# Nine small VectorE instructions placed ahead of one large one at each chunk boundary

## The chip, the cores and the metric

The kernel runs on one NeuronCore of one Trainium2 chip. The metric is device time in microseconds (us), median of the runs of one kernel. The engines are named as in the profile: PE is TensorE, DVE is VectorE, ACT is ScalarE, POOL is GpSimd, SP is SyncE; PEld is TensorE's weight load. Each engine takes its own instructions in the order in which they are written, and semaphores make it wait for others.

## The reference

128 samples of 750 x 32 values are cut into 92 overlapping patches each, embedded to 128 features, and sent through attention with 8 heads and a mixture of 8 experts of which each token uses 2. Cut to what matters:

```
h = patches(x) @ W + b                                # 128 x 92 tokens of 128 features
a = attention(layernorm(h))                           # 8 heads; a_flat is (tokens, 1024)
h = h + (a_flat @ Wlt)                                # the projection
t = layernorm(h)
logits = t @ Wr + br                                  # 8 experts
gates = softmax(logits); top 2, renormalised
out = h + sum over the 2 chosen e of gate_e * (relu(t @ W1[e] + b1[e]) @ W2[e] + b2[e])
```

## The kernel before, in words

It runs in four stages. The first computes embedding and attention, and leaves the attention result in device memory. The second, which the change touches, projects it, adds the residual, normalises, picks the two experts of each token and scatters the token rows to a sorted place in memory. The third runs the experts over tiles of 512 sorted rows, the fourth adds up.

The second stage takes the 11,776 tokens in 23 chunks of 512, numbered 0 to 22. Chunks 0 to 8 are written out, 9 to 20 are two chunks each in a loop that runs six times, 21 and 22 are written out again. While the chunk function works on chunk c, it also prepares and projects chunk c + 1:

- PE turns eight 512 x 128 blocks of chunk c + 1 (turn_a, L1546) and projects each one two places later (project). Blocks 0 to 5 are projected as high and low half, with three matmuls each (L342 to L344); blocks 6 and 7 in full precision (L1555). Between them stand the expert counts of chunk c - 1 (count, L1579 and L1581), and the turned residual and the logits of chunk c (turn_h L1566, logits L1573).
- ACT copies a turned block from PSUM as the rounded high half aT_h (L907), and makes the normalised rows trow (L924), the squares (L914) and the exponential for the gates (L937).
- DVE subtracts to get the low half aT_l (keep_aTl, L1147), adds the residual (keep_h1, L1157; the profile writes the tile as h), forms gates and row numbers of chunk c - 1 (weigh, L1223 to L1226, and rows_of, L1231 to L1236), and then runs the choice of experts for chunk c, a chain of small dependent instructions from L1183 to L1213 (shift, lg, top, eq, key, one, mask_line, upto).
- POOL scatters the rows of chunk c - 1 by eight indirect DMAs (L756), and takes the power for the deviation (root2, L747).

The waits around the change: PE's project(c + 1, 0) waits for the first low half; weigh waits for ACT's exponential and rows_of for PE's count; POOL's scatter waits for rows_of's last result posi (L1236); ACT's squares wait for DVE's lean (L1163); POOL's root2 waits for DVE's varB (L1168); DVE's shift (L1183) waits for root2. PE's turn_h waits for keep_h1, and keep_h1 waits for the last projection of its chunk. Every two chunks the transfers of arow and hch start as soon as keep_h1 has read hch.

Of the kernel before, what the change touches and what calls it, by code (L numbers as in the profile page):

```python
# [44 lines left out]
HL = 6  # L45
# [28 lines left out]
def at_least(eng, sem, value):  # L74

    if isinstance(value, int) and value <= 0:
        return
    eng.wait_ge(sem, value)
# [19 lines left out]
def build(nc, x, tok_w, tok_b, wq, wk, wv, wlt, wr, br, w1, b1, w2, b2, out):  # L98
# [8 lines left out]
    with ExitStack() as ctx, nc.allow_non_contiguous_dma("biases once"):  # L107
# [905 lines left out]
        def _(dve):  # L1013
# [130 lines left out]
            def keep_aTl(c, j):  # L1144
                at_least(dve, aTh_kept, AC * c + j + 1)
                at_least(dve, proj_done, AC * c + j - TURNS + 1)
                V.tensor_tensor(aT_l[:, j % TURNS], turn_ps[j % TURNS][:], aT_h[:, j % TURNS].bitcast(F32),  # L1147
                                ALU.subtract).then_inc(aTl_kept, 1)

            def keep_h1(c, i, q):  # L1150
                at_least(dve, proj_done, AC * (c + 1))
                if isinstance(c, int):
                    dve.wait_ge(a_in[q], 32 * (c // 2 + 1))
                else:
                    dve.wait_ge(a_in[q], 16 * (c - q + 2))
                at_least(dve, res_done, c - 1)
                V.tensor_tensor(h1[:, q].rearrange("d (r p) -> d r p", r=RT), proj_ps[:].rearrange("d (r p) -> d r p", r=RT),  # L1157
                                hch[q][:].rearrange("d (p r) -> d r p", r=RT), ALU.add).then_inc(h1_kept, 1)

            def keep_lean(c):  # L1160
                at_least(dve, lg_done, c + 1)
                at_least(dve, square_kept, 2 * c)
                V.tensor_copy(lean[:].unsqueeze(2), lg_ps[:, :, NE:NE + 1]).then_inc(lean_kept, 1)  # L1163

            def keep_var2(c):
                at_least(dve, square_kept, 2 * c + 2)
                at_least(dve, rstd2_kept, c)
                V.tensor_scalar(varB[:], varB[:], EPS, None, ALU.add).then_inc(var2_kept, 1)  # L1168
# [10 lines left out]
            def take_logits(c, q):  # L1179
                step_no[0] = 0  # L1180
                at_least(dve, trow_kept, 2 * c - 2)
                at_least(dve, rstd2_kept, c + 1)
                V.scalar_tensor_tensor(shift[:, q], lean[:], D ** 0.5, rstdB[:, q], ALU.mult, ALU.mult).then_inc(shift_kept, 1)  # L1183
                link(c, V.tensor_tensor(lg[:], lg_ps[:, :, 0:NE], wide(rstdB[:, q]), ALU.mult))
                link(c, V.tensor_tensor(lg[:], lg[:], brs[:].unsqueeze(1).to_broadcast([P, RT, NE]), ALU.add))

            def largest(c, which):

                m = top[:, which]
                link(c, V.tensor_reduce(m, lg[:], AX_X, ALU.max))  # L1190
                link(c, V.tensor_tensor(eq[:], lg[:], wide(m), ALU.is_equal))

            def first_of_equals(c, which):

                kk = top[:, 4 + which]
                link(c, V.tensor_tensor(key[:], eq[:], rank[:], ALU.mult))
                link(c, V.tensor_reduce(kk, key[:], AX_X, ALU.max))
                link(c, V.tensor_tensor(one[:, 1 - which], rank[:], wide(kk), ALU.is_equal))

            def without_first(c):  # L1200
                link(c, V.scalar_tensor_tensor(lg[:], one[:, 1], -3.0e38, lg[:], ALU.mult, ALU.add))

            def chosen(c):
                at_least(dve, count_done, c)
                step_no[0] += 1
                V.tensor_tensor(mask, one[:, 0], one[:, 1], ALU.add).then_inc(route, 1)
                V.tensor_tensor(top[:, 2], top[:, 1], top[:, 0], ALU.subtract).then_inc(gap_kept, 1)
                dve.wait_ge(route, NR * c + step_no[0])
                line = mask_line[:].bitcast(F32)
                windows = bass.AP(tensor=line.tensor, offset=line.offset,  # L1210
                                  ap=[list(line.ap[0]), [NE, RT], [1, NE], [NE, RT]])
                with nc.allow_low_precision("whole numbers up to 4"):
                    V.tensor_reduce(upto[:], windows, AX_X, ALU.add).then_inc(mask_kept, 1)  # L1213

            def weigh(c, q):

                at_least(dve, gapexp_kept, c + 1)
                at_least(dve, scattered[q], 16 * 2 * RT * (c // 2) if isinstance(c, int) else 8 * 2 * RT * (c - q))
                dve.wait_ge(goal_kept, SETUP)
                gate = [trow[:, q, choice, :, D + 1:D + 2] for choice in (0, 1)]  # L1220
                ratio = top[:, 3].unsqueeze(2)
                mine = trow[:, q, :, :, D:D + 1].bitcast(I32)
                link(c, V.tensor_scalar(top[:, 6], top[:, 3], 1.0, None, ALU.add))  # L1223
                link(c, V.reciprocal(gate[1], top[:, 6].unsqueeze(2)))
                V.tensor_scalar(mine, mine, 2 * CT, None, ALU.add)
                V.tensor_tensor(gate[0], gate[1], ratio, ALU.mult)  # L1226

            def rows_of(c, q):

                at_least(dve, count_done, c + 1)  # L1230
                link(c, V.tensor_tensor(place[:], count_ps[:, 64:64 + RT * NE].rearrange("p (r e) -> p r e", r=RT),  # L1231
                                        base[:].unsqueeze(1).to_broadcast([P, RT, NE]), ALU.add))
                link(c, V.tensor_tensor(base[:], count_ps[:, 64 + RT * NE:64 + (RT + 1) * NE], base[:], ALU.add))
                link(c, V.tensor_tensor(seat[:], one[:], place[:].unsqueeze(1).to_broadcast([P, 2, RT, NE]), ALU.mult))
                link(c, V.tensor_reduce(posf[:], seat[:], AX_X, ALU.add))
                V.tensor_copy(posi[:, q], posf[:]).then_inc(posi_kept, 1)  # L1236
# [11 lines left out]
            def first_tiles_ready():  # L1248

                lined = [0]  # L1250

                def nxt(ins):
                    lined[0] += 1
                    ins.then_inc(ready_kept, 1)
                    dve.wait_ge(ready_kept, lined[0])

                nxt(V.tensor_tensor(held[:], base[0:1], ebase[0:1], ALU.subtract))
                nxt(V.tensor_reduce(least[:, 0:1], held[:], AX_X, ALU.min))
                nxt(V.tensor_scalar(least[:, 1:2], least[:, 0:1], float(TT), -16.0 * 2 * RT, ALU.is_ge, ALU.mult))
                for half in (0, 1):  # L1260
                    V.tensor_scalar(ready[:, half:half + 1], least[:, 1:2], 16.0 * 2 * RT * ((NCH + 1 - half) // 2), None,
                                    ALU.add).then_inc(ready_kept, 1)
# [3 lines left out]
            def chunk(c, i, q, more):  # L1266
                after_first = not isinstance(c, int) or c > 0
                keep_h1(c, i, q)
                for j in range(AC):
                    if j == 4:  # L1270
                        keep_var2(c)
                    if more and j < HL:
                        keep_aTl(c + 1, j)
                    if j == 0 and after_first:
                        step_no[0] = CHOSEN
                        weigh(c - 1, 1 - q)
                        rows_of(c - 1, 1 - q)
                        if isinstance(c, int) and c == NCH - 2:
                            first_tiles_ready()
                        assert step_no[0] == NR, step_no  # L1280
                    if j == 1:
                        keep_lean(c)
                    if isinstance(c, int) and 1 <= c <= NE and j == 2:
                        dve.wait_ge(high_kept, NE + c)
                        V.tensor_tensor(w2split[:, c - 1, :, 1], w2raw[:, c - 1, :, 1], w2split[:, c - 1, :, 0].bitcast(F32),
                                        ALU.subtract).then_inc(low_kept, 1)
                    if j == 5:
                        take_logits(c, q)
                        largest(c, 0)
                    if j == 6:  # L1290
                        first_of_equals(c, 0)
                        without_first(c)
                        largest(c, 1)
                    if j == AC - 1:
                        first_of_equals(c, 1)
                        chosen(c)
                        assert step_no[0] == CHOSEN, step_no
# [395 lines left out]
```

## Time and profile before

| what | value |
|---|---|
| median of 3 runs | 1533.73 us (1533.18 to 1535.3) |
| the profiled execution's own time | 1533.04 us |
| its span in the trace | 1530.9 us |
| second stage in the trace, first to last keep_h1 | 843.19 to 1109.46 us |
| busy in the span: PE, PEld, DVE, ACT, POOL | 92%, 74%, 77%, 66%, 52% |
| mean granted TensorE clock | 0.963 |

The profile is of one execution, whose span is 2.1 us shorter than its own time. Shares of busy time are averages over four stages with different limits, so a change in the second is read from rows of the second. In a row of the timeline stand the start, the duration, the engine, the line, the operation with its tiles, and in brackets the idle time of the engine before it with what ended it.

### The profile page before, as it was taken

The page shows a single profiled execution, that of the slowest core. Times are in us where ns is not written, and L with a number is a line of the kernel's source. Part 1 is how long each engine was busy: PE and PEld are TensorE (multiplying, and loading weights), DVE is VectorE, ACT ScalarE, POOL GpSimd, SP SyncE. Part 2 cuts the span into 40 slices and gives each one's busy share as a digit, 9 for nine tenths or more (in the row PEclk, how much of TensorE's full clock was granted, in tenths as well). Part 3 has the DMA queues.
Part 4 walks back from the last instruction along what each step waited for, and adds up shares of the span by engine and source line. Part 5 has one row for each costly group of instructions (what it writes and reads, how often), then busy time and mean ns, then how long its engine had stood idle before and what let it go on. Part 6 is the DMA issues. An engine that isn't in the chain of part 4 may idle for free.

```text
span 1530.9 us, 31767 instructions
## 1 busy us (share of the span) xinstructions
PE 1401.2 (92%) x7902; PEld 1132.8 (74%) x7902; DVE 1180.4 (77%) x3082; ACT 1017.2 (66%) x2282; POOL 801.9 (52%) x891
## 2 busy tenths in 40 slices
PE   4899999999999999999998999999969999999930
PEld 3687888887888888888886777777758888888820
DVE  1899898988989898898995688888856666666633
ACT  1587887878788788888885677777745555555510
POOL 1476443444444444444442377777765666666665
PEclk8999999999999999999998999999979999999975
DMA  3322222222223222222224887777477777777667
GB/s 83 131 75 90 76 101 81 89 84 78 89 74 107 79 85 86 77 89 83 100 106 162 290 267 268 241 256 254 171 274 243 248 247 246 247 245 247 244 211 297
DMA packets 115925, 249.58 MB, mean 163 GB/s; under 512 B 15504, under 2 KB 70944, under 8 KB 112928
## 3 DMA queue, kind: packets, MB, share of 16 engines
q1 hardware_dynamic: 94640, 209.63, 38.6%
q0 software_dynamic: 14368, 32.25, 6.6%
q10 hardware_dynamic: 6864, 7.09, 1.3%
q8 instruction: 22, 0.36, 0.1%
q14 instruction: 31, 0.25, 0.1%
HBM read 100.78 MB, written 92.56 MB: 126 GB/s over the span
## 4 chain that ended last, share of the span: by engine, by line
PE 73%; DMA 9%; DVE 6%; issue 5%; POOL 4%; ACT 2%; SPq 1%; POOLq 0%; DVEq 0%; ACTq 0%
PE bank L342 16%; PE bank L344 15%; PE bank L343 15%; PE bank L1481 9%; PE bank L1414 5%; PE bank L1506 5%; DMA hch<-h_scratch 3%; DMA sorted_scratch<-trow,posi 2%; POOL sorted_scratch L756 2%; PE bank L1404 2%; PE bank L1618 2%; PE bank L1643 1%; DMA out_dram<-outs 1%; PE bank L1546 1%; PE bank L1422 1%
## 5 line engine op out<-in xcount | busy, mean ns | idle before, releaser
L628 POOL TENSOR_TENSOR prob<-expo,inv 92x368 f32<-92x368 f32 x256 | 204.6, 799 | 422.6 <-DVE inv L1106 422.6
L783 POOL DMA_INDIRECT y_scratch<-ytok,tin x212 | 205.0, 967 | 137.6 <-issue 72.1
L1351 DVE SCALAR_TENSOR_TENSOR hid_l<-bank,hid_h 128x512 fp32r<-128x512 f32 x212 | 146.4, 691 | 128.6 <-ACT hid_h L969 125.3
L969 ACT ACTIVATE hid_h<-bank 128x512 fp32r<-128x512 f32 x212 | 126.7, 598 | 149.3 <-PE bank L344 149.3
L756 POOL DMA_INDIRECT sorted_scratch<-trow,posi x184 | 180.4, 980 | 71.4 <-issue 62.6
L1481 PE MATMUL bank<-z,xnT 128*92 128x368 f32 x512 | 200.3, 473 | 0.0
L1099 DVE TENSOR_REDUCE peak<-bank 92x4 f32<-92x368 f32 x256 | 136.3, 532 | 77.5 <-PE bank L1481 77.4
L830 ACT ACTIVATE z<-bank 128x368 f32<-128x368 f32 x256 | 122.0, 477 | 66.7 <-PE bank L344 59.2
L868 ACT ACTIVATE w2s<-bank 128x368 fp32r<-128x368 f32 x256 | 122.4, 478 | 45.8 <-PE bank L344 41.1
L875 ACT ACTIVATE expo<-cent 92x368 f32<-92x368 f32 x256 | 130.2, 508 | 31.4 <-DVE cent L1111 28.9
L1126 DVE TENSOR_TENSOR w2s<-bank,w2s 128x368 fp32r<-128x368 f32 x256 | 136.2, 532 | 5.4 <-ACT w2s L868 2.5
L1111 DVE TENSOR_TENSOR cent<-bank,peak 92x368 f32<-92x368 f32 x256 | 136.6, 533 | 1.0
L1119 DVE TENSOR_TENSOR probT_l<-bank,probT_h 92x368 fp32r<-92x368 f32 x256 | 134.9, 527 | 1.8 <-ACT probT_h L856 1.8
L1092 DVE TENSOR_REDUCE total<-expo 92x4 f32<-92x368 f32 x256 | 133.6, 522 | 0.5 <-ACT expo L875 0.3
L884 ACT ACTIVATE val<-bank 128x368 f32<-128x368 f32 x256 | 120.4, 470 | 17.8 <-PE bank L344 16.6
L1506 PE MATMUL bank<-ident,prob 92*92 92x92 f32 x1024 | 123.0, 242 | 0.3 <-POOL prob L628 0.3
L342 PE MATMUL bank<-probT_h,xtok_h 92*128 92x368 f32 x256 | 114.1, 446 | 9.9 <-DVE w2s L1126 7.1
L856 ACT ACTIVATE probT_h<-bank 92x368 fp32r<-92x368 f32 x256 | 119.8, 468 | 0.3
L1546 PE MATMUL bank<-ident,arow 128*128 128x128 f32 x736 | 114.7, 280 | 4.5 <-DMA hch<-h_scratch 4.4
L1506 PEld LDWEIGHTS bank<-ident,prob 92*92 92x92 f32 x1024 | 103.4, 124 | 18.5 <-issue 5.5
L1546 PEld LDWEIGHTS bank<-ident,arow 128*128 128x128 f32 x736 | 91.3, 146 | 34.6 <-DMA hch<-h_scratch 11.7
L1147 DVE TENSOR_TENSOR aT_l<-bank,aT_h 128x512 fp32r<-128x512 f32 x138 | 94.7, 691 | 27.4 <-ACT aT_h L907 25.5
(193 smaller groups left out, 3803.0 us busy)
## 6 DMA issues: line engine op xcount, KB each, us to landing
ax_scratch<-val SPq DMA_DIRECT2D x64, 736.0 KB, 3.5
arow<-ax_scratch SPq DMA_DIRECT2D x23, 2048.0 KB
w1t<-w1s SPq DMA_DIRECT2D x53, 512.0 KB, 3.5
w2t<-w2s SPq DMA_DIRECT2D x53, 512.0 KB, 3.1
tin<-sorted_scratch SPq DMA_DIRECT2D x53, 260.0 KB, 3.0
xin<-in_x_dram SPq DMA_DIRECT2D x32, 372.0 KB
yearly<-y_scratch SPq DMA_DIRECT2D x24, 256.0 KB, 9.0
h_scratch<-hT SPq DMA_DIRECT2D x32, 184.0 KB, 7.1
```

Of the source, the lines that this page charges most:

```text
L342: mm(dst, wh, vh, start=start, stop=False)
L343: mm(dst, wh, vl, start=False, stop=False)
L344: return mm(dst, wl, vh, start=False, stop=stop)
L628: nc.gpsimd.tensor_tensor(prob[:, k % 2], expo[:, k % 2], inv[:, k % 2].unsqueeze(2).to_broadcast([S, HH, S]), ALU.mult).then_inc(prob_kep ...
L756: pool.indirect_dma_start(out=sorted_dram, out_offset=bass.IndirectOffsetOnAxis(ap=posi[:, q, choice, r:r + 1], axis=0), in_=trow[:, q, ch ...
L783: pool.indirect_dma_start(out=y_dram, out_offset=bass.IndirectOffsetOnAxis(ap=tin[:, b, r, D:D + 1].bitcast(I32), axis=0), in_=ytok[:, b % ...
L1099: V.tensor_reduce(peak[:, k % 2], sc, AX_X, ALU.max).then_inc(peak_kept, 1)
L1111: V.tensor_tensor(cent[:, k % 2], sc, peak[:, k % 2].unsqueeze(2).to_broadcast([S, HH, S]), ALU.subtract).then_inc(cent_kept, 1)
L1351: V.scalar_tensor_tensor(hid_l[:, f], hid_ps[f][:], 0.0, hid_h[:, f].bitcast(F32), ALU.max, ALU.subtract).then_inc(hidl_kept, 1)
L1481: mm(score_ps[k % 2][0:S, 0:GT], xnT[:, q, b * S:(b + 1) * S], z[:, b, half * HH:(half + 1) * HH, :], start=True, stop=True).then_inc(scor ...
L1506: ins = nc.tensor.transpose(probT_ps[kt % 2][0:S, m * S:(m + 1) * S], prob[:, kt % 2, m], ident[0:S, 0:S])
L1546: ins = nc.tensor.transpose(turn_ps[j % TURNS][:, r * P:(r + 1) * P], arow[q][:, r, j * P:(j + 1) * P], ident[:])
```

## The change

At the start of the chunk function on VectorE, the subtraction for block 0 of the next chunk is issued after weigh and rows_of instead of ahead of them. Blocks 1 to 5 stay where they are. Line numbers behind it grow by two.

```
@@ -1269,7 +1269,7 @@
                 for j in range(AC):
                     if j == 4:
                         keep_var2(c)
-                    if more and j < HL:
+                    if more and 0 < j < HL:
                         keep_aTl(c + 1, j)
                     if j == 0 and after_first:
                         step_no[0] = CHOSEN
@@ -1278,6 +1278,8 @@
                         if isinstance(c, int) and c == NCH - 2:
                             first_tiles_ready()
                         assert step_no[0] == NR, step_no
+                    if more and j == 0:
+                        keep_aTl(c + 1, j)
                     if j == 1:
                         keep_lean(c)
```

The first place is VectorE at the start of an early chunk, before the change. The row with h is keep_h1, the aT_l rows are low halves of blocks 0 and 1.

```order
L1213 TENSOR_REDUCE upto<-mask_line 128x32
L1157 TENSOR_TENSOR h<-bank,hch 128x512
L1147 TENSOR_TENSOR aT_l<-bank,aT_h 128x512
L1223 TENSOR_SCALAR top<-top 128x4
L1224 RECIPROCAL trow<-top 128x4
L1225 TENSOR_SCALAR trow<-trow 128x8
L1226 TENSOR_TENSOR trow<-trow,top 128x4
L1231 TENSOR_TENSOR place<-bank,base 128x32
L1233 TENSOR_TENSOR base<-bank,base 128x8
L1234 TENSOR_TENSOR seat<-one,place 128x64
L1235 TENSOR_REDUCE posf<-seat 128x8
L1236 CAST posi<-posf 128x8
```

The same place with the change:

```order
L1157 TENSOR_TENSOR h<-bank,hch 128x512
L1223 TENSOR_SCALAR top<-top 128x4
L1224 RECIPROCAL trow<-top 128x4
L1225 TENSOR_SCALAR trow<-trow 128x8
L1226 TENSOR_TENSOR trow<-trow,top 128x4
L1231 TENSOR_TENSOR place<-bank,base 128x32
L1233 TENSOR_TENSOR base<-bank,base 128x8
L1234 TENSOR_TENSOR seat<-one,place 128x64
L1235 TENSOR_REDUCE posf<-seat 128x8
L1236 CAST posi<-posf 128x8
L1147 TENSOR_TENSOR aT_l<-bank,aT_h 128x512 x2
L1163 COPY lean<-bank 128x4
```

Block 0's low half has moved behind nine small instructions and now stands directly before block 1's (the x2); h, lean and all that follows keep their order. This holds for chunks 1 to 21: chunk 0 has no gates to form, and chunk 22 has no next chunk.

The second place is VectorE at the start of chunk 21, before the change, where the four lines of first_tiles_ready (held, least, ready) follow rows_of:

```order
L1236 CAST posi<-posf 128x8
L1257 TENSOR_TENSOR held<-base,ebase 1x8
L1258 TENSOR_REDUCE least<-held 1x1
L1259 TENSOR_SCALAR least<-least 1x1
L1261 TENSOR_SCALAR ready<-least 1x1 x2
L1147 TENSOR_TENSOR aT_l<-bank,aT_h 128x512
L1163 COPY lean<-bank 128x4
```

And with the change:

```order
L1236 CAST posi<-posf 128x8
L1257 TENSOR_TENSOR held<-base,ebase 1x8
L1258 TENSOR_REDUCE least<-held 1x1
L1259 TENSOR_SCALAR least<-least 1x1
L1261 TENSOR_SCALAR ready<-least 1x1 x2
L1147 TENSOR_TENSOR aT_l<-bank,aT_h 128x512 x2
L1163 COPY lean<-bank 128x4
```

In chunk 21 block 0's low half stands behind these five instructions too. On PE, ACT, POOL and SP the order is unchanged.

## Rows read from the trace of the kernel before

**Rows 1.** Two stretches; busy of PE, PEld, DVE, ACT, POOL; clock; DMA share, GB/s:
```profile
869.00:884.00 15.00, 14.62 (x72) 12.29 (x73) 11.21 (x38) 9.46 (x25) 10.73 (x12) 0.77 0.68 233
955.00:1037.00 82.00, 78.42 (x476) 61.64 (x475) 68.93 (x244) 59.35 (x152) 62.09 (x70) 1.00 0.69 246
```

**Rows 2.** Timeline of DVE, chunk 9 and on to chunk 11:
```profile
955.62 1.08 DVE L1157 TENSOR_TENSOR h<-bank,hch 128x512 f32<-128x512 f32 x1
956.68 0.69 DVE L1147 TENSOR_TENSOR aT_l<-bank,aT_h 128x512 fp32r<-128x512 f32 x1
957.29 0.16 DVE L1223 TENSOR_SCALAR top<-top 128x4 f32<-128x4 f32 x1
...
958.97 0.69 DVE L1147 TENSOR_TENSOR aT_l<-bank,aT_h 128x512 fp32r<-128x512 f32 x1
...
962.27 1.36 DVE L1147 TENSOR_TENSOR aT_l<-bank,aT_h 128x512 fp32r<-128x512 f32 x2 [0.31 <-ACT aT_h L907]
963.59 0.16 DVE L1183 SCALAR_TENSOR_TENSOR shift<-lean,rstdB 128x4 f32<-128x4 f32 x1
...
967.18 1.08 DVE L1157 TENSOR_TENSOR h<-bank,hch 128x512 f32<-128x512 f32 x1
...
979.04 1.08 DVE L1157 TENSOR_TENSOR h<-bank,hch 128x512 f32<-128x512 f32 x1 [0.31 <-issue]
```

**Rows 3.** Timeline of PE, chunk 9:
```profile
956.95 0.63 PE L1566 MATMUL bank<-ident,h 128*128 128x128 f32 x4 [0.39 <-DVE h L1157]
...
958.62 0.48 PE L342 MATMUL bank<-aT_h,wlt_h 128*128 128x512 f32 x1
...
959.75 0.48 PE L342 MATMUL bank<-aT_h,wlt_h 128*128 128x512 f32 x1
...
961.67 0.60 PE L1546 MATMUL bank<-ident,arow 128*128 128x128 f32 x4
```

**Rows 4.** Timeline of ACT, chunk 9, the copies of blocks 4 and 5:
```profile
961.63 1.29 ACT L907 ACTIVATE aT_h<-bank 128x512 fp32r<-128x512 f32 x2
```

**Rows 5.** Timeline of DVE, start of chunk 22:
```profile
1109.46 1.04 DVE L1157 TENSOR_TENSOR h<-bank,hch 128x512 f32<-128x512 f32 x1
1110.42 0.16 DVE L1223 TENSOR_SCALAR top<-top 128x4 f32<-128x4 f32 x1
```

**Rows 6.** Timelines of PE in chunks 2 and 7, DVE and PE in chunk 13:
```profile
873.90 0.78 PE L342 MATMUL bank<-aT_h,wlt_h 128*128 128x512 f32 x1
...
934.84 0.48 PE L342 MATMUL bank<-aT_h,wlt_h 128*128 128x512 f32 x1
...
936.42 0.47 PE L342 MATMUL bank<-aT_h,wlt_h 128*128 128x512 f32 x1 [0.21 <-DVE aT_l L1147]
...
1005.58 0.48 PE L342 MATMUL bank<-aT_h,wlt_h 128*128 128x512 f32 x1
...
1006.34 0.69 DVE L1147 TENSOR_TENSOR aT_l<-bank,aT_h 128x512 fp32r<-128x512 f32 x1
...
1007.08 0.50 PE L342 MATMUL bank<-aT_h,wlt_h 128*128 128x512 f32 x1
```

**Rows 7.** Who waited for the low halves L1147 (us, times):
```profile
  PE bank L342: 1.4, 5
  PEld bank L342: 0.6, 2
```

**Rows 8.** Timeline of DVE: shift in chunks 1, 5 and 21:
```profile
865.71 0.16 DVE L1183 SCALAR_TENSOR_TENSOR shift<-lean,rstdB 128x4 f32<-128x4 f32 x1 [3.30 <-POOL rstdB L747]
...
916.07 0.16 DVE L1183 SCALAR_TENSOR_TENSOR shift<-lean,rstdB 128x4 f32<-128x4 f32 x1 [0.56 <-POOL rstdB L747]
...
1105.93 0.16 DVE L1183 SCALAR_TENSOR_TENSOR shift<-lean,rstdB 128x4 f32<-128x4 f32 x1 [0.87 <-POOL rstdB L747]
```

**Rows 9.** Timeline of POOL: root2 in chunk 10:
```profile
973.88 1.04 POOL L747 TENSOR_TENSOR rstdB<-varB,power 128x4 f32<-128x4 f32 x1 [0.27 <-DVE varB L1168]
```

**Rows 10.** Instructions on posi: engines sat idle before them until (us, times):
```profile
  DVE posi L1236: 3.8, 5
```

More of the change, by code:

```diff
@@ L1271, in chunk @@
                         keep_var2(c)
-                    if more and j < HL:
+                    if more and 0 < j < HL:
                         keep_aTl(c + 1, j)
@@ L1280, in chunk @@
                         assert step_no[0] == NR, step_no
+                    if more and j == 0:
+                        keep_aTl(c + 1, j)
                     if j == 1:
```

## The prediction

> **What bounds the kernel now.** I read the table of stretches first: from 955 to 1037 us, which are seven chunks of the second stage, PE is busy for 78.42 of 82 us at a granted clock of 1.00, DVE for 84%, POOL for 76% [rows 1]. No engine is full, so the stage is set by a loop of waits, and I looked for it in the timelines of one chunk. The reader is to follow chunk 9 [rows 2 to 4]. keep_h1 starts at 955.62. PE's turn_h waits for it and starts at 956.95, 1.33 behind; then come the logits and one more turn, and PE reaches project 0 at 958.62, 3.00 behind the start of keep_h1. From there PE runs without a gap to the turn of block 5, 961.67 to 962.27; ACT has copied that block by 961.63 + 1.29 = 962.92; DVE's low half of it starts in the same instant (962.27 + 0.69 = 962.96) and ends at 963.63; shift starts at 963.59 with no idle time before it, and the chain of small instructions runs to the next keep_h1 at 967.18, which shows no idle time either. So the loop closes: 3.00 from keep_h1 to project 0 and 8.56 from project 0 to the next keep_h1, 11.56 in all, with DVE at work for the last 4.2 us of it (962.96 to 967.18). Of each pair in the loop the second step to the next pair costs 0.30 more, which stands in front of keep_h1 as issue time at the branch (979.04 - 967.18 = 11.86) [rows 2].
>
> The low half of block 0 is not on that loop today: it ends at 956.68 + 0.69 = 957.37, and PE comes for it at 958.62. It has 1.25 us to spare [rows 2, 3].
>
> **The change, part by part.** It adds no instruction and no transfer; it moves one DVE instruction of 0.69 us behind nine small ones.
>
> 1. The nine small ones go from 957.29 to 958.97, the start of the next large one: 1.68 us [rows 2]. The low half of block 0 is late by this, less what it frees.
>
> 2. When do the nine start without the low half ahead of them? Chunk 22 has no next chunk and shows it already: L1223 follows keep_h1 at 1110.42 - 1109.46 = 0.96 [rows 5]. In the loop the first instruction after keep_h1 stands at 956.68 - 955.62 = 1.06 [rows 2]. I take 1.03, between the two.
>
> 3. The low half of block 0 then ends 1.03 + 1.68 + 0.69 = 3.40 behind the start of keep_h1. PE needs some 0.05 more: in chunk 13, where PE waits for the low half of block 1, that ends at 1006.34 + 0.69 = 1007.03 and PE starts at 1007.08 [rows 6]. So project 0 starts at 3.45 instead of 3.00: **PE is late by 0.45 us per chunk.** The 1.25 us to spare are used up, and 1.70 - 1.25 gives the same 0.45. The bounds are 0.38 (0.96 at the start) and 0.51 (PE needing 0.08 more and 1.06 at the start).
>
> 4. Does it come back later in the chunk? Behind project 0 PE has no idle time in which to catch up, so the turn of block 5 ends at 962.72 instead of 962.27. ACT had its copy of block 4 behind it by then (961.63 + 0.65), so its copy of block 5 ends at about 963.35, and DVE's low half at 964.08 instead of 963.63. shift starts as much later, and so does the next keep_h1. Nothing in the chain from shift to upto waits, so nothing gives. PE's own way, project 0 to last projection to keep_h1, is delayed alike. The loop becomes 12.01.
>
> 5. What keeps its time: the low half of block 1 ends where it did, since the sum of the work ahead of it is the same; lean, the squares, varB and root2 hang on it and stay at their distance from keep_h1. Posi comes about 0.61 us earlier (the distance between 956.68 and 957.29), so POOL may scatter sooner. POOL waited for posi 5 times, 3.8 us in all [rows 10], but its root2 is held by varB, not by the scatters, in most chunks of the loop (0.27 idle in front of it) [rows 9]. Earlier scatters are therefore worth nothing there. Behind the moved instruction on DVE nothing is queued that gets later; behind PE's new wait is everything PE does in the chunk, and ACT and DVE wait for that.
>
> 6. The new wait replaces older ones. PE already waited 7 times for a low half, 2.0 us together [rows 7], always at block 1: the low half of block 0 stood waiting for ACT and pushed the nine and block 1 back. In chunk 7 project 1 follows project 0 by 936.42 - 934.84 = 1.58, against 959.75 - 958.62 = 1.13 in chunk 9: 0.45 lost. In chunk 13 it is 1007.08 - 1005.58 = 1.50, 0.37 lost [rows 3, 6]. With the nine in front, that wait of DVE is filled, and the loss at block 1 goes.
>
> The sum over the 21 chunks from 1 to 21:
> - Chunks 1 and 2: nothing. In chunk 1 shift waits 3.30 us for POOL [rows 8]. In chunk 2 PE runs at a lower granted clock (0.77 over the stretch) and comes to project 0 only at 873.90, when block 0's low half would long be there [rows 1, 6].
> - Chunks 3 to 8: about nothing together. Chunk 3 pays 0.45. In chunk 4 the input transfer is late and the nine fill DVE's wait, which I estimate to give the 0.45 back. In chunks 5 and 6 shift waits 0.56 for POOL (one of two such rows) [rows 8], which covers 0.45. Chunks 7 and 8 lose 0.45 at block 1 now, and lose it at block 0 then.
> - Chunks 9 to 19: 11 x 0.45 = 4.95, less 0.37 in chunk 13 and about 0.2 in chunk 16 (a wait of the same kind, half as long) = 4.4 us.
> - Chunks 20 and 21: chunk 20 pays 0.45. In chunk 21 five more instructions stand ahead of block 0, but shift waits 0.87 for POOL there [rows 8], which takes back chunk 20's delay. Net nothing. After it POOL leads to the end of the stage, and all later work is shifted by the same amount.
>
> The sum is +4.4 us on the profiled 1533.04, which is 1537.4. That execution was 0.7 us under the median of 1533.73, so against the median I expect 1533.73 + 4.4 = 1538.1.
>
> **A rule against the change.** PE gets a fresh pause of some 0.45 us in every chunk. From 955 to 1037 PE idles for 3.6 of 82 us in short pauses at a granted clock of 1.00, its full level of 2.4 GHz; chunk 2, from 869 on, has 0.77, part of it at 1.2 GHz [rows 1]. The Trainium skill, TensorE: Matmul & The Clock Gate, section A second HAM failure mode: psum-queue depth-cycling, says that small idle times between groups of matmuls, if frequent, can make the clock swing between full and half. By that rule each chunk could cost far more than its 0.45 us. The trace so far speaks against it. It is the last rival below, priced from rows.
>
> **The rivals.**
> - *Full price.* Each of the 21 chunks pays, nothing is hidden: 21 x 0.45 = 9.5 us, 1543.2. For it: the loop is closed, and a later chunk could lose what an earlier one saved. Against it: the waits for POOL and for block 1 stand in the trace.
> - *Hidden.* PE makes up the 0.45, because ACT and DVE find the blocks later than they need them, or POOL's scatters set the pace: 1533 to 1535, say 1534. For it: ACT's copy of block 5 and DVE's low half before it end within 0.04 us of each other, so small shifts may vanish. Against it: this slack is 0.04, not 0.45, and root2 waits for varB.
> - *Faster: the filled wait decides.* The place is the boundary where ACT's copy of block 0 is late because its trow rows waited for scatters. There the nine run in DVE's idle time, posi comes earlier, the scatters end earlier, and the next trow rows do too. It would give the 2.0 us of PE's waits [rows 7] and at most the 3.8 us of POOL's waits [rows 10]; I price it at 2.5 us, 1531.2. It decides if more than half of the chunks start with a late block 0. For it: seven chunks show the wait. Against it: in the other fourteen there is nothing to fill, and these pay.
> - *The clock falls.* Chunk 2, at the lower clock, shows the size: its L342 takes 0.78 against 0.48 [rows 3, 6]. 18 such matmuls by 0.30 in 18 chunks are over 90 us if it stayed so; a fifth of that is 1553.
>
> **How the numbers follow.** Forecast 0.57, full price 0.14, hidden 0.18, faster 0.09, clock 0.02. The likeliest gives 1538.1, with its own range from 1536.3 to 1540. A measurement of this kernel tells about 0.2% from no change, 3.1 us: slower means above 1536.8, faster below 1530.7. Of the forecast 0.52 lies above 1536.8 and 0.05 below it; with full price and clock, slower is 0.68. Same is 0.05 + 0.18 + some of the faster case (its 2.5 us is inside the bound), 0.24. Faster is 0.08. The range for 8 in 10 runs from 1533.2, which takes in most of the hidden case, to 1543.0, which takes in most of the full price.
>
> **What would show it.** In the profile after, in a loop chunk: L1225 (the old L1223) starts about 1.0 behind keep_h1; the low half of block 0 about 2.7 behind; project 0 at 3.45 with a bracket of PE waiting for aT_l, in about 11 or more chunks; keep_h1 to keep_h1 12.0 and 12.3 in turn instead of 11.56 and 11.86; posi 2.5 behind keep_h1 instead of 3.2. The last keep_h1 is 4.4 us later than 1109.46. PE's waits for block 1, POOL's long waits for root2's input excepted, are gone. Step 4 is wrong if project 0 is late but keep_h1 keeps its 11.56; step 3 is wrong if project 0 stays at 3.0; step 6 is wrong if chunks 4, 7, 8 and 13 each grow by 0.45. The prediction fails if the second stage changes by less than 3 or more than 7 us, or if stages one, three or four move.

## The result, and the profile after

The changed kernel takes 1538.7 us (median of 16 runs, 1535.19 to 1544.06), the kernel before 1533.86 us (16 runs, 1530.05 to 1547.6). The ratio is 1.0029, 95% interval 1.0016 to 1.0042: slower by 0.3%. The forecast was 1538.1 in a range of 1533.2 to 1543.0. One slow run (1634.47 us at a mean clock of 0.831, of the kernel with the change in chunks 1 to 8 alone) is left out of the ratios below.

The profiled execution with the change has a span of 1533.1 us, 2.2 more than before. That is less than the times say, and the two spans cut at the first and the last keep_h1 show why. The columns are us, busy us (and instructions) of PE, PEld, DVE, ACT and POOL, granted clock, DMA share and GB/s; the first row is the second stage before, the second row is the same stage with the change.

```profile
843.19:1109.46 266.27, 251.24 (x1494) 196.38 (x1491) 220.32 (x774) 192.32 (x492) 189.40 (x201) 0.99 0.72 251
841.82:1113.98 272.16, 253.35 (x1494) 197.15 (x1491) 219.50 (x774) 193.97 (x492) 190.56 (x201) 0.99 0.69 245
```

The instructions are the same in number and busy for nearly the same time, in a stage that is 5.9 us longer. What lies ahead of it was 1.4 us shorter in this execution and what follows 2.3 us, 3.7 in all. Two executions of the kernel before differ there by 1.3 and 0.7 us, and in the two further profiles with the change the first keep_h1 is at 842.85 and 842.11, with 421.7 and 421.4 us behind the last against 421.4 before. So this is scatter, and I compare the second stage by itself.

The timeline of DVE in chunk 9, with the change, answers to [rows 2]:

```profile
955.91 1.09 DVE L1157 TENSOR_TENSOR h<-bank,hch 128x512 f32<-128x512 f32 x1
956.90 0.17 DVE L1223 TENSOR_SCALAR top<-top 128x4 f32<-128x4 f32 x1
...
958.59 1.29 DVE L1147 TENSOR_TENSOR aT_l<-bank,aT_h 128x512 fp32r<-128x512 f32 x2
959.79 0.15 DVE L1163 COPY lean<-bank 128x4 f32<-128x4 f32 x1
...
963.68 0.69 DVE L1147 TENSOR_TENSOR aT_l<-bank,aT_h 128x512 fp32r<-128x512 f32 x1 [0.39 <-ACT aT_h L907]
964.29 0.15 DVE L1183 SCALAR_TENSOR_TENSOR shift<-lean,rstdB 128x4 f32<-128x4 f32 x1
...
967.91 1.12 DVE L1157 TENSOR_TENSOR h<-bank,hch 128x512 f32<-128x512 f32 x1
...
980.29 1.10 DVE L1157 TENSOR_TENSOR h<-bank,hch 128x512 f32<-128x512 f32 x1 [0.32 <-issue]
```

The nine small instructions start 0.99 behind keep_h1, the low half of block 0 2.68 behind, and the steps are 12.00 and 12.38 us where they were 11.56 and 11.86. In front of block 5's low half there is now a wait of 0.39 for ACT where there was none. PE and ACT in the same chunk, answering to [rows 3, 4]:

```profile
957.24 0.63 PE L1568 MATMUL bank<-ident,h 128*128 128x128 f32 x4 [0.39 <-DVE h L1157]
...
959.33 0.50 PE L342 MATMUL bank<-aT_h,wlt_h 128*128 128x512 f32 x1 [0.18 <-DVE aT_l L1147]
...
963.04 0.60 ACT L907 ACTIVATE aT_h<-bank 128x512 fp32r<-128x512 f32 x1 [0.48 <-PE bank L1548]
```

turn_h is where it was, 1.33 behind keep_h1. project 0 has a wait for the low half in front of it and stands at 3.42. The bracket says 0.18 only, because it counts from the modelled end of the turn ahead; the start is what counts. ACT, whose copies of blocks 4 and 5 were back to back, now waits 0.48 for PE ahead of block 5: the delay travels from PE through ACT to DVE's chain, as the steps of the prediction say. The view of who waited for the low halves has these lines in place of the two of [rows 7]:

```profile
  PE bank L342: 6.5, 19
  PEld bank L342: 5.5, 12
```

By the first line, PE waits in nineteen of the 21 chunks, at block 0 and no longer at block 1. The two others are chunk 2 and chunk 4. In every looped chunk project 1 now follows project 0 by 1.15 to 1.17 us.

The parts of the stage in all profiled executions, in us from keep_h1 to keep_h1, and what was timed (the ratio is to runs of the kernel before on the same chip):

| kernel | chunks 0-2 | 3-8 | 9-20 | 21 | falls of the clock in 9-20 | ratio (95%) |
|---|---|---|---|---|---|---|
| before | 40.2 | 72.2 | 140.7 | 13.1 | 0 | |
| before, again | 40.0 | 71.5 | 140.6 | 13.0 | 0 | |
| with the change | 40.1 | 74.0 | 145.6 | 12.5 | 0 | 1.0029 (1.0016 to 1.0042) |
| with the change, again | 41.6 | 72.1 | 148.7 | 12.5 | 2 | |
| with the change, third | 39.9 | 73.1 | 147.2 | 12.5 | 1 | 1.003 (1.0016 to 1.0043) |
| behind four of nine | 39.7 | 71.1 | 140.3 | 13.1 | 0 | 0.9993 (0.9973 to 1.0013) |
| behind seven of nine | 40.2 | 71.6 | 142.7 | 13.2 | 0 | 1.0003 (0.9985 to 1.0022) |
| change in 9 to 20 alone | 40.4 | 74.5 | 146.3 | 13.1 | 0 | 1.0049 (1.0023 to 1.0076) |
| change in 1 to 8 alone | 40.2 | 71.5 | 140.9 | 13.0 | 0 | 0.9998 (0.9974 to 1.0021) |
| change in 21 alone | 40.3 | 75.6 | 140.3 | 12.6 | 0 | |
| change, PE one turn later | 40.3 | 71.0 | 139.9 | 12.6 | 0 | 0.9968 (0.9951 to 0.9986) |
| before, PE one turn later | 40.1 | 71.5 | 140.8 | 13.0 | 0 | 0.9991 (0.9978 to 1.0003) |
| the last version below | 38.0 | 70.2 | 138.6 | 13.2 | 0 | 0.996 (0.9941 to 0.9979) |

Two kernels have a fall in chunks 3 to 8, each after a long wait of PE for a late input: it is in the 74.5 of the change in 9 to 20 alone (chunk 4 takes 16.22) and in the 75.6 of the change in 21 alone (chunk 7 takes 16.04). The 41.6 is chunk 2 with 15.56 instead of 14.18, because the granted clock stayed low there for some 10 us instead of 7.

### The profile page after: what moved, and what is told of

It reads as the page before. It is cut to its first block, busy times and chain, and to the rows that moved or that the text cites. A ratio compares the mean times of both kernels' runs of the same rounds, so it can differ in the third digit from the quotient of the medians.

```text
span 1533.1 us, 31767 instructions
## 1 busy us (share of the span) xinstructions
PE 1402.5 (91%) x7902; PEld 1133.1 (74%) x7902; DVE 1183.1 (77%) x3082; ACT 1020.0 (67%) x2282; POOL 804.0 (52%) x891
## 4 chain that ended last, share of the span: by engine, by line
PE 76%; DVE 10%; DMA 6%; issue 4%; ACT 2%; POOL 1%; SPq 1%; DVEq 0%; POOLq 0%; ACTq 0%
PE bank L342 17%; PE bank L344 15%; PE bank L343 15%; PE bank L1483 9%; PE bank L1416 5%; PE bank L1508 5%; PE bank L1548 2%; PE bank L1406 2%; PE bank L1620 2%; PE bank L1645 1%; DMA xin<-in_x_dram 1%; DMA out_dram<-outs 1%; DMA yearly<-y_scratch 1%; DVE aT_l L1147 1%; DMA hch<-h_scratch 1%
## 5 line engine op out<-in xcount | busy, mean ns | idle before, releaser
L342 PE MATMUL bank<-probT_h,xtok_h 92*128 92x368 f32 x256 | 114.1, 446 | 9.8 <-DVE w2s L1126 7.1
L1147 DVE TENSOR_TENSOR aT_l<-bank,aT_h 128x512 fp32r<-128x512 f32 x138 | 93.1, 689 | 35.0 <-ACT aT_h L907 28.0
```

Of the source, the lines that this page charges most:

```text
L342: mm(dst, wh, vh, start=start, stop=False)
```

## The experiments

**How far two executions differ.** The kernel before, unchanged.

> The kernel before, unchanged, profiled once more: how far do two executions differ? Theory: the loop chunks 9 to 20 take 140.7 us within 0.5, since a loop of fixed durations sets them; chunks 3 to 8 differ by up to 1.5 us, since input transfers end some of their waits; the first, third and fourth stage differ by 1 to 3 us, which is the scatter between runs. Rival: the loop chunks scatter as much as the change, 3 us or more, and the comparison of two profiles says nothing.

Measured: 140.64 us for chunks 9 to 20, against 140.70; 71.5 against 72.2 for chunks 3 to 8. The four profiles whose looped chunks have the order of before (these two and two further down) have 140.34 to 140.92 us for chunks 9 to 20: a difference of 1 us in the looped part can be read, one of 0.5 us cannot. Late inputs make a looped chunk now and then 0.3 to 0.7 us longer, and one of chunks 3 to 8 more often and by more.

**Four of the nine.** The low half of block 0 between weigh and rows_of:

```
                         weigh(c - 1, 1 - q)
+                        if more:
+                            keep_aTl(c + 1, 0)
                         rows_of(c - 1, 1 - q)
...
-                    if more and j == 0:
+                    if more and j == 0 and not after_first:
                         keep_aTl(c + 1, j)
```

The second cut takes it out of its place behind the nine.

> The low half of block 0 stands between weigh and rows_of: four small instructions ahead of it instead of nine. Theory (PE's project 0 has 1.25 us to spare, and only what exceeds it costs): the delay is 0.57 us, under the spare, so in the loop chunks project 0 stays at 3.00 behind keep_h1, keep_h1 to keep_h1 at 11.56 and 11.86, first to last keep_h1 at 266 us like before (within 1.5), and the time is that of before, ratio 0.999 to 1.001. Rival (each small instruction put ahead costs its share, 4/9 of the change): project 0 at 3.2, the stage 2.5 us longer, ratio 1.0013. Rival (the first wait of weigh for ACT's exponential is what hurts): as much as the change, stage 5 us longer.

Measured: 140.31 us for chunks 9 to 20, ratio 0.9993 (0.9973 to 1.0013). The timelines of DVE and PE in chunk 9:

```profile
952.01 1.09 DVE L1157 TENSOR_TENSOR h<-bank,hch 128x512 f32<-128x512 f32 x1
...
953.62 0.69 DVE L1147 TENSOR_TENSOR aT_l<-bank,aT_h 128x512 fp32r<-128x512 f32 x1
...
955.01 0.48 PE L342 MATMUL bank<-aT_h,wlt_h 128*128 128x512 f32 x1
```

The low half starts 1.61 behind keep_h1 instead of 1.06 and project 0 stays at 3.00. A delay of 0.55 costs nothing, so the price isn't in proportion, and a wait of weigh for the exponential isn't the cause either, since weigh is ahead here too.

**Seven of the nine.** The same between seat and posf, inside rows_of:

```
                 link(c, V.tensor_tensor(seat[:], one[:], ...
+                if low:
+                    keep_aTl(nxt, 0)
                 link(c, V.tensor_reduce(posf[:], seat[:], AX_X, ALU.add))
```

> The low half of block 0 stands behind seven of the nine small instructions (behind seat, ahead of posf). Theory: the delay is 1.24 us less 0.03, just at the spare of 1.25, so project 0 is at 3.0 to 3.05 in the loop chunks and the stage is within 1.5 us of before; the last two small instructions carry the whole price of the change. Rival (price in proportion): 7/9 of 0.45, project 0 at 3.35, stage 4.2 us longer than before, ratio 1.0025.

Measured: project 0 at 3.16 to 3.33, chunks 9 to 20 in 142.65 us, 2.0 longer than before; ratio 1.0003 (0.9985 to 1.0022). In chunk 9:

```profile
955.01 1.10 DVE L1157 TENSOR_TENSOR h<-bank,hch 128x512 f32<-128x512 f32 x1
...
957.45 0.69 DVE L1147 TENSOR_TENSOR aT_l<-bank,aT_h 128x512 fp32r<-128x512 f32 x1 [0.21 <-DVE seat L1234]
...
958.20 0.50 PE L342 MATMUL bank<-aT_h,wlt_h 128*128 128x512 f32 x1
```

Both numbers missed, and the row says why. Before the change posf starts 0.26 behind the start of seat; here the large instruction starts 0.44 behind it (seat stands at 957.01), after an idle time of 0.21. So the low half starts at 2.44, not 2.27, and takes up more than the spare. Why the gap behind seat is larger ahead of this instruction isn't shown. Counted with it the spare of 1.25 holds: the delay is 2.44 - 1.06 = 1.38, which is 0.13 past the spare, and with the 0.05 that PE needs project 0 should stand at 3.18; it stands at 3.19. The three points lie on a line with a kink: a delay of 0.55 moves project 0 by nothing, of 1.38 by 0.19, of 1.62 by 0.42, and the looped chunks grow by 0, 0.16 and 0.41 us each on average.

**PE one turn later, with the change.** One number: PE projects a block three turns behind instead of two, so that it turns block 3 while it waits for the low half of block 0.

```
-LAG_P = 2
+LAG_P = 3
```

> The change as it is, but PE projects each block three turns behind instead of two, so that project 0 stands behind the turn of block 3. Theory (the late low half costs only because project 0 stands in front of the turns on PE, whose copies the choice of experts waits for): PE has the turn of block 3 to do while it waits, the turn of block 5 ends before ACT needs it, shift is back at 7.9 to 8.0 behind keep_h1 and keep_h1 to keep_h1 at 11.6 and 11.9: the stage is 4 to 6 us shorter than with the change, like before. Rival (the delay of VectorE's own order is what costs): nothing comes back, steps stay at 12.0 and 12.3.

Measured: 139.9 us for chunks 9 to 20, 5.7 less than with the change, ratio to before 0.9968 (0.9951 to 0.9986): the loss is gone, and a little more. In chunk 9, DVE and PE:

```profile
954.32 1.08 DVE L1157 TENSOR_TENSOR h<-bank,hch 128x512 f32<-128x512 f32 x1 [0.24 <-PE bank L1557]
...
956.92 1.07 PE L1548 MATMUL bank<-ident,arow 128*128 128x128 f32 x8
957.75 0.50 PE L342 MATMUL bank<-aT_h,wlt_h 128*128 128x512 f32 x1
...
962.11 0.15 DVE L1183 SCALAR_TENSOR_TENSOR shift<-lean,rstdB 128x4 f32<-128x4 f32 x1
```

project 0 is as late as with the change, 3.43 behind keep_h1. But blocks 2 and 3 are turned ahead of it (the x8), shift is at 7.79, and the step is 11.53. The low half's lateness doesn't cost by itself; it costs where PE has nothing else to do and the turns that DVE's chain needs stand behind it. keep_h1 waits 0.24 for PE's last projection here; it does so at the start of four of the twelve looped chunks (0.15 to 0.32), so PE's own way and DVE's chain are now about equally long.

**PE one turn later, without the change.** The same number in the kernel before.

> The kernel before (low half of block 0 ahead of the nine) with PE projecting three turns behind. It separates the two edits in the version that was faster. Theory: project 0 stands at 3.4 behind keep_h1 whatever VectorE's order is, so this kernel and the changed one with three turns behind take the same time: chunks 9 to 20 in 139.9 us within 0.6, and the gain against before is the lag's, ratio 0.997 to 0.999. Rival: the new order is worth something once it costs nothing (it fills the waits for late inputs), and this kernel is 1 to 3 us slower than the changed one with the lag.

Measured: 140.83 us for chunks 9 to 20 (one of them 12.24 by a late input), 0.3 more than the theory allowed, ratio 0.9991 (0.9978 to 1.0003). In chunk 11, an undisturbed one:

```profile
979.21 1.07 DVE L1157 TENSOR_TENSOR h<-bank,hch 128x512 f32<-128x512 f32 x1 [0.31 <-issue]
...
982.63 0.48 PE L342 MATMUL bank<-aT_h,wlt_h 128*128 128x512 f32 x1
...
987.18 0.16 DVE L1183 SCALAR_TENSOR_TENSOR shift<-lean,rstdB 128x4 f32<-128x4 f32 x1
```

project 0 stands at 3.42 with no late low half at all, as late as with the change, and the step is 11.52: a late project 0 is no cost where the turns stand ahead of it. Undisturbed steps are 11.52 to 11.55 and 11.70 to 11.84, with both orders the same within 0.1. Whether the new order is worth something beside the lag, as the rival says, stays open: the two ratios were measured on different chips, their intervals overlap, and the stage is 1.6 us longer than with the changed order, of which late inputs can make as much.

**Which chunks pay.** The change in the looped chunks alone, and in chunks 1 to 8 alone:

```
-                    if more and 0 < j < HL:
+                    if more and (0 < j < HL or j == 0 and not (not isinstance(c, int))):
...
-                    if more and j == 0:
+                    if more and j == 0 and (not isinstance(c, int)):
```

and for the second `isinstance(c, int) and c <= 8` as the condition.

> The change in the looped chunks 9 to 20 alone; 0 to 8 and 21 keep the old order. Theory: these chunks carry the price: 12 x 0.45 less what filled waits give back, so chunks 9 to 20 take 4 to 5 us more than before (145 instead of 140.7), chunks 1 to 8 nothing more; ratio 1.0027 to 1.0033. Rival (the price is spread evenly over 21 chunks): 12/21 of it, 2.7 us, ratio 1.0017.

> The change in chunks 1 to 8 alone. Theory of the prediction: late input transfers, POOL and the old waits at block 1 cover it, so chunks 3 to 8 take 0 to 1 us more than before, ratio 1.000 to 1.0007. Rival, from the profile with the change (chunks 3, 7 and 8 each 0.34 to 0.44 longer, chunk 4 0.6 longer by a later transfer): 1.8 us more, ratio 1.0012, or 1.2 if the later transfer was chance.

Measured: with the looped chunks alone 146.25 us in 9 to 20, which is 5.6 more than before, 0.5 of it in chunk 11 with a late input. The ratio is 1.0049 (1.0023 to 1.0076), above what either theory said; the interval reaches down to the change's own. With chunks 1 to 8 alone, chunks 3 to 8 took 71.45 us, as in the two profiles of before (72.2 and 71.5), and the ratio is 0.9998 (0.9974 to 1.0021). So the looped chunks carry the price.

The steps show that an early chunk pays too when nothing disturbs it. With the old order the shortest early steps are 11.30, 11.34 and 11.41 us (chunks 3, 5 and 8 of the kernel with the change in 9 to 20 alone); with the new order they are 11.80 to 11.83 (chunks 3, 4, 6 and 7 here), 0.45 more. The sum stays because most early chunks of the kernel before are at 11.8 to 12.7 already, through late copies of block 0 and waits for POOL.

**Chunk 21 alone.** The condition is `c == NCH - 2`.

> The change in chunk 21 alone, where five more instructions stand ahead of block 0. Theory: project 0 comes at 4.05 behind keep_h1 instead of 2.84, and nothing comes of it, because shift waited 0.87 us for POOL: keep_h1 of chunk 21 to that of chunk 22 stays at 13.1 within 0.15, with shift's wait at 0.1 to 0.5. Rival: the step grows by 0.3 to 1.2 us, as PE is late by that.

Measured in one profile: 12.64 us, shorter than 13.14 and 12.98. Both theories missed. project 0 stands at 4.20 and PE is late by 1.4, and still the step shrinks. Chunk 21 in the kernel before, and then with the change in it alone:

```profile
1096.32 1.09 DVE L1157 TENSOR_TENSOR h<-bank,hch 128x512 f32<-128x512 f32 x1
...
1099.62 0.17 DVE L1236 CAST posi<-posf 128x8 int32<-128x8 f32 x1
...
1103.79 0.97 POOL L756 DMA_INDIRECT sorted_scratch<-trow,posi  x1 [2.24 <-DVE varB L1168]
1104.79 1.04 POOL L747 TENSOR_TENSOR rstdB<-varB,power 128x4 f32<-128x4 f32 x1
```

```profile
1097.80 1.07 DVE L1157 TENSOR_TENSOR h<-bank,hch 128x512 f32<-128x512 f32 x1
...
1100.44 0.17 DVE L1236 CAST posi<-posf 128x8 int32<-128x8 f32 x1
...
1102.00 0.47 PE L342 MATMUL bank<-aT_h,wlt_h 128*128 128x512 f32 x1 [1.14 <-DVE aT_l L1147]
...
1104.78 0.96 POOL L756 DMA_INDIRECT sorted_scratch<-trow,posi  x1 [1.88 <-issue]
1105.76 1.05 POOL L747 TENSOR_TENSOR rstdB<-varB,power 128x4 f32<-128x4 f32 x1
...
1106.91 0.16 DVE L1183 SCALAR_TENSOR_TENSOR shift<-lean,rstdB 128x4 f32<-128x4 f32 x1
```

root2 starts 7.96 behind keep_h1 instead of 8.31 to 8.47. Two scatters stand ahead of it on POOL, and the second of them keeps its distance from posi: it starts 4.17 us behind it in the kernel before and 4.34 here, and root2 starts 5.15 to 5.32 us behind posi in chunk 21 of all thirteen profiles, whatever the order. posi came 0.5 to 0.66 sooner, shift waits no more, and the step is 0.35 to 0.5 us shorter. POOL idles about 2 us between the two scatters; what it waits for there no trace says (the bracket names varB in one and nothing in the other).

**How often the clock falls.** The changed kernel, profiled twice more.

> The kernel with the change, profiled once more. Theory: chunks 9 to 20 take 145.6 us within 0.5 again, 12.0 and 12.3 in turn; the input of chunk 5, which came 2.08 us behind keep_h1 in the first profile, comes at another time, and chunk 4 is shorter than 13.27. Rival: the late transfer is caused by the change and is there again within 0.3 us.

> The kernel with the change once more, to see how often the clock falls inside the loop. Clock theory (the pause of PE ahead of project 0 makes it fall in some executions, as in 2 of 12 loop chunks of the second profile): one or more of the loop chunks 9 to 20 shows a granted clock under 0.95 and takes 1.3 to 1.6 us more, and the timed runs at lower mean clock are the slower ones. Rival (these two falls were chance, like the falls after late inputs in other kernels): all twelve at 1.00, chunks 9 to 20 in 145.6 us within 0.6. The ratio to before is 1.003 to 1.005 either way.

Measured: chunks 9 to 20 took 148.73 us in the second profile and 147.18 in the third, 3.1 and 1.6 more than in the first: the first theory missed by its 145.6, and the clock theory came in. In chunk 4 PE waited for the late input for 2.21 us in the first profile, not at all in the second and 1.43 us in the third, so that lateness was chance. The ten timed runs of the third set (1537.16 to 1539.98) have mean clocks of 0.962 to 0.964, too alike to say whether the slower ones are those with a fall. The excess stands in chunks 11 and 19 of the second profile and chunk 15 of the third, with 13.60, 13.60 and 13.76 us instead of 12.0. The table of stretches around chunk 11 of the second:

```profile
972.00:984.00 12.00, 11.27 (x68) 8.73 (x68) 9.56 (x35) 8.47 (x22) 8.86 (x9) 1.00 0.67 238
984.00:987.00 3.00, 2.82 (x10) 2.32 (x10) 1.53 (x4) 1.96 (x7) 1.94 (x2) 0.60 0.91 377
987.00:990.00 3.00, 3.00 (x16) 2.40 (x15) 1.55 (x3) 1.82 (x7) 1.55 (x2) 0.83 0.93 386
```

and PE there:

```profile
982.13 0.63 PE L1568 MATMUL bank<-ident,h 128*128 128x128 f32 x4 [0.73 <-DVE h L1157]
...
984.22 0.50 PE L342 MATMUL bank<-aT_h,wlt_h 128*128 128x512 f32 x1 [0.18 <-DVE aT_l L1147]
...
984.56 0.57 PE L343 MATMUL bank<-aT_l,wlt_h 128*128 128x512 f32 x1
...
986.06 0.78 PE L342 MATMUL bank<-aT_h,wlt_h 128*128 128x512 f32 x1
```

PE pauses ahead of turn_h as it does in the kernel before (0.73 in both), and again ahead of project 0; within the next matmuls the granted clock goes from 2.4 to 1.2 GHz (L342 takes 0.78 instead of 0.48) and comes back some 3 us later. Each fall costs about 1.6 us. All three stand in the first chunk of a pair, where the pause ahead of turn_h is the longest (0.66 to 0.73, against about 0.4 in the second). Four profiles have project 0 later by 0.4 in the looped chunks with nothing for PE to do meanwhile (the three of the changed kernel and the change in 9 to 20 alone): 3 falls in their 48 looped chunks. The nine other profiles have none in 108. This suggests that the new pause makes the clock fall, and does not show it: three falls are few, and no run has the pause without the rest of the change.

**A version that beats both.** The low half of block 0 between weigh and rows_of, lean straight behind rows_of, PE one turn later, and the residual turned behind block 2:

```
-LAG_P = 2
+LAG_P = 3
...
                         weigh(c - 1, 1 - q)
+                        if more:
+                            keep_aTl(c + 1, 0)
                         rows_of(c - 1, 1 - q)
+                        keep_lean(c)
...
-                    if more and j == 0:
+                    if more and j == 0 and not after_first:
                         keep_aTl(c + 1, j)
-                    if j == 1:
+                    if j == 1 and not after_first:
                         keep_lean(c)
...
-                    if j == 1:
+                    if j == 2:
                         turn_h(c, q)
                         logits(c, q)
```

> A version meant to beat both: low half of block 0 between weigh and rows_of, lean straight behind rows_of and ahead of block 1, PE projects three turns behind and turns the residual after block 2 instead of after block 1. Theory (what is left in the loop is PE's pause of 0.35 to 0.7 before it turns the residual, and the wait of the squares for lean): PE fills the pause with the turn of block 2, the steps become 11.2 to 11.4 and 11.5 to 11.7, chunks 9 to 20 take 137 to 138.5 us, ratio 0.995 to 0.997. Rival (POOL, eight scatters of 1.27 and root2, sets 11.4 at best, or the branch of the loop stays in front): as with the lag alone, 139.5 to 140.

Measured: 1526.56 us, ratio 0.996 (0.9941 to 0.9979), 6 us under the kernel before and 12 under the changed one on the same chip. Chunks 9 to 20 take 138.6 us, a little over what was expected. The steps are 11.3 to 11.4 and 11.5 to 11.7 where no input is late. DVE at the start and in the middle of chunk 9:

```profile
953.00 0.39 DVE L1236 CAST posi<-posf 128x8 int32<-128x8 f32 x1
953.10 0.29 DVE L1163 COPY lean<-bank 128x4 f32<-128x4 f32 x1
...
957.66 0.16 DVE L1183 SCALAR_TENSOR_TENSOR shift<-lean,rstdB 128x4 f32<-128x4 f32 x1 [0.41 <-POOL rstdB L747]
```

lean comes 0.7 earlier, at 3.27 behind keep_h1, and shift waits 0.41 for POOL's root2, as it does for 0.27 to 0.41 in every looped chunk. POOL, which had time to spare, is the next bound, as the rival named, though at steps of 11.3 and not at those of the version with the lag alone. The version has several edits at once; what each is worth was not measured.

## Why the prediction was right, point by point

- *The loop of waits* (keep_h1, turn_h, project 0, block 5, the chain, keep_h1) was read rightly. The step went from 11.56 to 12.00 where the prediction said 12.01.
- *Steps 1 to 3*, project 0 at 3.45: measured 3.42 to 3.49 in eleven of the twelve looped chunks, 3.60 in chunk 15. The start of the nine was 0.98 to 1.05, where I took 1.03. (The prediction calls their first line L1225; it stands ahead of the edit and is L1223 in both kernels.)
- *Step 4*, nothing comes back: shift moved by 0.37 to 0.54 behind keep_h1 in the ten looped chunks that had no late input before. The two versions with PE one turn later show that the position of project 0 ahead of the turns is the reason.
- *Step 5*: posi came 2.5 behind keep_h1 as said, and was worth nothing in the loop. In chunk 21 it was worth 0.35 to 0.5 us. The prediction expected chunk 21 to take back only what chunk 20 lost.
- *Step 6*: the losses at block 1 went. Chunk 13 grew by 0.09 and chunk 16 by 0.28, where the sum had 0.08 and 0.25. Chunks 7 and 8 came out 0.3 to 0.4 longer all the same. In chunk 7 the first of the nine takes 0.38 instead of 0.16, and the nine 1.84 instead of 1.58 us:

```profile
931.87 0.97 POOL L756 DMA_INDIRECT sorted_scratch<-trow,posi  x1 [0.30 <-issue]
932.43 0.38 DVE L1223 TENSOR_SCALAR top<-top 128x4 f32<-128x4 f32 x1
```

  In the kernel with the change in chunks 1 to 8 alone the same instruction takes 0.17 there, and the step is 11.81:

```profile
930.05 0.97 POOL L756 DMA_INDIRECT sorted_scratch<-trow,posi  x1 [0.30 <-issue]
931.04 0.17 DVE L1223 TENSOR_SCALAR top<-top 128x4 f32<-128x4 f32 x1
```

  The difference is the scatter that POOL is at. In the first case L1223 starts 0.56 us behind the start of a scatter and ends with it (932.81 against 932.84); in the second the scatter is over. The thirteen profiles agree without an exception: the 63 times that L1223 starts 0.54 to 0.74 us behind the start of a scatter it takes 0.20 to 0.40 us and ends 0.02 to 0.04 us before the scatter does; at any other place it takes 0.14 to 0.25. In all three profiles of the changed kernel this happens in chunks 7, 8 and 15, in two of them in chunk 6, and now and then elsewhere. With the low half behind the nine it delays project 0, to 3.65 to 3.68 in chunks 6 to 8 and to 3.60 in chunk 15.
- *The sum.* It was +4.4, all of it in chunks 9 to 21; the first profile has +4.2 (4.90 in 9 to 20, less 0.67 in chunk 21). Without their falls the other two have the same in 9 to 20, 145.5 us. For chunks 3 to 8 it had about nothing. The profiles with the change have 74.0, 72.1 and 73.1, those without it in these chunks and without a fall of the clock 72.2, 71.5, 71.1 (behind four of nine) and 71.5 (before with PE one turn later): about 1.2 to 1.5 us more, in part by late inputs and in part by the stretched L1223, and the kernel with the change there alone has 71.5.
- *The clock* was the term that was mis-sized. The prediction gave it a chance of 0.02 and priced it as lasting, at 1553. What the runs show is rare and short: 3 falls in 36 looped chunks of the changed kernel, about 1.6 us each, which is 1.6 us per execution on average. The Trainium skill's page weighed in the prediction (TensorE: Matmul & The Clock Gate, A second HAM failure mode) describes such swings after frequent short idle times. The traces are in keeping with it, in single short falls and not in the size that I had worked out.
- *How near the number came* is in part luck. The three profiles with the change have a second stage of 272.2, 274.9 and 272.7 us, the two of before 266.3 and 265.1: 7.5 us more on average, from 4.9 in the looped chunks, 1.6 from falls, 1.2 in chunks 3 to 8, some 0.4 in chunks 0 to 2, and -0.6 in chunk 21. The second profile, 8.6 above that of before, lies beyond the 7 us that the prediction itself had set as a sign of being wrong, through its two falls (3.2 us). The medians say 4.8 us (2.5 to 6.4 by the interval), and 6.0 in the set of the third profile. The mechanism and the 0.44 per chunk are shown; that the sum of 4.4 lies so near the 4.8 is not proof of its smaller terms, and why the profiled executions differ by more than the medians stays open.

## What to carry to other kernels

An instruction can be put behind others for nothing as long as its consumer comes later than its new end; measure that distance in the timeline (1.25 us here) against the duration of what it is put behind, gaps included, because one step past it everything is paid in every turn of the loop. If the consumer is an engine in order, ask what stands behind the waiting instruction: giving that engine one more independent piece ahead of the wait took the whole price away (139.9 us against 145.6 and 140.7). Earlier results for an engine that waits for something else are worth nothing, and in the one place where it hangs on just these they are worth about what they are early.

## What the runs showed of the hardware that was not expected

Pauses of PE of 0.66 to 0.73 us ahead of turn_h and 0.18 to 0.36 us ahead of project 0, some 1.9 us apart, were followed by a fall of the granted clock to 1.2 GHz for about 3 us in 3 of 48 looped chunks; the same pauses in other chunks were not.

Single waits for a late input behave as unevenly. PE in chunk 4 of the first profile with the change, and in chunk 4 of the kernel with the change in the loop alone:

```profile
895.98 0.66 PE L1548 MATMUL bank<-ident,arow 128*128 128x128 f32 x4 [2.21 <-DMA hch<-h_scratch]
```

```profile
896.61 0.66 PE L1548 MATMUL bank<-ident,arow 128*128 128x128 f32 x4 [1.92 <-DMA hch<-h_scratch]
```

The longer one was followed by no fall, and the chunk took 13.27 us. The shorter one was followed by a clock of 0.50 for some 7 us, of which this row shows four, and the chunk took 16.22 us, 3 us more:

```profile
898.00:902.00 4.00, 4.00 (x19) 3.81 (x18) 2.77 (x13) 2.14 (x5) 2.23 (x3) 0.50 1.00 353
```

A wait of 2.41 us in chunk 7 of the kernel with the change in chunk 21 alone had a fall as long behind it, with a step of 16.04. So nearly the same pause costs 1.6 to 3 us more or nothing. This may be much of the scatter between runs of one kernel: of the 16 runs of the changed kernel the fastest (1535.19) has a mean clock of 0.967 and the slowest (1544.06) 0.961. Which of them had such a fall wasn't recorded.

The other is the small instruction of step 6: on VectorE L1223, 0.16 us long, ends only with POOL's scatter when it starts 0.54 to 0.74 us into it. That is a coincidence in time in all thirteen traces; no run moved the scatter to test it.
